# A slot-routing stage: the moments of one input taken a group earlier in each engine's queue

## The reference, cut to what matters

```python
x = x + mamba_layers(_layernorm(x), ...)      # ends in layernorm(r, norm_f_w, norm_f_b)
x = x + slots(_layernorm(x), ...)             # the first slot stage
x = x + attention(_layernorm(x), ...)
x = x + slots(_layernorm(x), ...)             # the second slot stage

def slots(x, ...):
    ctx = concatenate([x, slot_mean])
    h = gelu(ctx @ w1.T + b1)
    logits = (h @ w2.T + b2) / (abs(tau) + 0.1)
    alpha = top-8 softmax of logits over 64 slots
    slot_input = einsum('bts,btd->bsd', alpha, x) / alpha.sum(1)
    S_new = gru(slot_input, slots)
    return einsum('bts,bsd->btd', alpha, S_new @ wv.T + bv) @ wo.T + bo
```

## Time and profile before

| | us |
|---|---|
| median of 3 runs | 2447.85 (2445.73 to 2450.03) |
| the profiled execution, its own time | 2445.1 |
| its span in the profile | 2443.3 |
| first slot stage in it, from the end of Mamba to the start of attention | about 1765 to 1925 |
| second slot stage | from about 2349 |
| busy over the span: PE, DVE, ACT, POOL | 2114.9, 1886.0, 1785.2, 1636.1 |

### The profile page before, as it was taken

One profiled execution on the slowest core, in us unless ns is written; L12 is line 12 of the kernel. 1 busy time (PEld: TensorE's weight loads), 2 busy tenths in 40 slices (PEclk: granted clock), 3 DMA queues, 4 the chain that ended last, 5 costly groups with the idle time before them and its releaser, 6 DMA issues. The chain is left out here.

```text
span 2443.3 us, 40627 instructions
## 1 busy us (share of the span) xinstructions
PE 2114.9 (87%) x14680; PEld 1256.1 (51%) x14680; DVE 1886.0 (77%) x2590; ACT 1785.2 (73%) x3059; POOL 1636.1 (67%) x1436
## 2 busy tenths in 40 slices
PE   5989899898988989899898989988527599999977
PEld 2545545454554545455454554544324367666655
DVE  6888889888898888889888898988566455556555
ACT  3989898988989898998889889898333144444442
POOL 2888989898898988889898898989622123112120
PEclk9999999999999999999999999999857789999989
DMA  7240413405052341414324051331050301111032
GB/s 240 61 122 14 121 58 78 107 25 122 18 122 65 105 109 31 122 44 96 81 51 114 17 122 51 88 88 43 10 186 0 128 19 38 32 35 32 21 124 69
DMA packets 129788, 183.75 MB, mean 75 GB/s; under 512 B 14002, under 2 KB 75954, under 8 KB 129204
## 3 DMA queue, kind: packets, MB, share of 16 engines
q1 hardware_dynamic: 129588, 181.16, 27.6%
HBM read 134.45 MB, written 42.47 MB: 72 GB/s over the span
## 5 line engine op out<-in xcount | busy, mean ns | idle before, releaser
L620 POOL TENSOR_TENSOR h<-h,C_rep 128x512 f32<-128x512 f32 x1024 | 1275.5, 1280 | 195.2 <-ACT h_carry L529 195.2
L404 DVE TENSOR_TENSOR_SCAN h<-decay,h_carry,psum 128x512 f32<-128x512 f32 x768 | 955.4, 1269 | 126.8 <-PE psum L751 95.7
L521 ACT ACTIVATE decay<-dt_rep,A 128x512 f32<-128x512 f32 x1024 | 729.1, 712 | 97.3 <-DVE h L404 93.9
L751 PEld LDWEIGHTS psum<-ident,u_B 128*128 128x128 f32 x4096 | 478.9, 142 | 558.5 <-DVE h L404 306.6
L751 PE MATMUL psum<-ident,u_B 128*128 128x128 f32 x4096 | 632.9, 281 | 137.5 <-DVE h L404 105.5
L543 ACT ACTIVATE u_B<-u_tok,B_tok 128x512 f32<-128x512 f32 x832 | 588.9, 709 | 64.0 <-PE psum L751 46.3
L404 DVE TENSOR_TENSOR_SCAN h<-decay,zero,psum 128x512 f32<-128x512 f32 x256 | 318.6, 1269 | 50.0 <-PE psum L751 34.5
L762 PE MATMUL psum<-h,state_sum 128*32 128x512 f32 x2048 | 282.6, 625 | 10.9 <-POOL h L620 10.5
L609 POOL TENSOR_TENSOR u_B<-u_tok,B_tok 128x512 f32<-128x512 f32 x192 | 200.3, 1043 | 19.1 <-DVE u_tok L375 19.1
L674 PE MATMUL psum<-x_dt_gated,tap_diag 128*128 128x512 f32 x384 | 189.2, 597 | 0.0
L1578 DVE TENSOR_REDUCE a_row_max<-a_psum 128x4 f32<-128x512 f32 x128 | 87.7, 685 | 127.3 <-PE a_psum L1719 127.3
(11 more groups left out here) (207 smaller groups left out, 2757.3 us busy)
## 6 DMA issues: line engine op xcount, KB each, us to landing
dt_rep<-dt_rows SPq DMA_DIRECT2D x256, 256.0 KB, 5.6
C_rep<-C_rows SPq DMA_DIRECT2D x256, 64.0 KB, 2.0
dt_rows<-x_dt_gated SPq DMA_DIRECT2D x32, 512.0 KB, 5.0
residual<-mamba_residual SPq DMA_DIRECT2D x16, 512.0 KB, 3.9
mamba_residual<-residual SPq DMA_DIRECT2D x16, 512.0 KB, 2.9
x_tok<-mamba_residual SPq DMA_DIRECT2D x15, 512.0 KB, 4.5
f_gru_weights<-in_slot_gru_dram SPq DMA_DIRECT2D x2, 2176.0 KB
u_B<-in_x_dram SPq DMA_DIRECT2D x8, 512.0 KB, 9.3
```

Source lines behind the costliest of these rows:

```text
L404: dve.tensor_tensor_scan(h[:, slot(u)], dec[:, u % DEC], PS[:, u % 2], first, ALU.mult, ALU.add)\
L521: act.activation(dec[:, u % DEC], dtr[:, k % EG], ACT.Exp, scale=A[:, s // STEPS, k:k + 1]).then_inc(S["decay"], 1)
L620: pool.tensor_tensor(h[:, slot(u)], h[:, slot(u)], crep[:, k // EG], ALU.mult).then_inc(S["hc"], 1)
L751: ins = pe.transpose(PS[:, u % 2, tb * P:(tb + 1) * P], pr[:, f % 2, tb, eg], ident[:])
```

## The change

It changes the order of work in the first slot stage only. The moments of r of a group are now taken by DVE one group earlier than before, so that two groups of r are ahead at any time: `r_moments(0)` and `r_moments(1)` at the start, `r_moments(2)` before `combine(1)`, `r_moments(3)` before `combine(2)`. Two tables give the index of the moments in the new order, `R_AT` = 0, 1, 3, 5 for r and `X_AT` = 2, 4, 6, 7 for x. POOL serves the moments in that order. On ACT, `norm_r(1)` stands before `norm_x(0)`, and `norm_r(g + 2)` before `norm_x(g + 1)`. Without `normed` the order is as before.

```diff
+    R_AT = [max(2 * g - 1, 0) for g in range(G)]
+    X_AT = [min(2 * g + 2, 2 * G - 1) if normed else g for g in range(G)]
...
                 def norm_x(g):
-                    n = PER * g + PER - 1
+                    n = X_AT[g]
...
                 for g in range(G):
-                    for n in range(PER * g, PER * (g + 1)):
-                        rstd(n)
+                    if normed:
+                        for r in range(2) if g == 0 else range(g + 1, min(g + 2, G)):
+                            rstd(R_AT[r])
+                    rstd(X_AT[g])
                     norm_x(g)
...
                 def r_moments(g):
                     if g < G:
-                        moments(2 * g, rr, g, r_ld)
+                        moments(R_AT[g], rr, g, r_ld)
...
-                        moments(2 * g + 1, xa, g, None)
+                        moments(X_AT[g], xa, g, None)
...
                 if normed:
                     r_moments(0)
+                    r_moments(1)
                 else:
                     combine(0)
...
                 if normed:
-                    r_moments(1)
+                    r_moments(2)
                 combine(1)
-                if normed:
-                    r_moments(2)
                 dve.wait_ge(S["b2"], 1)
                 for g in range(G):
+                    if normed:
+                        r_moments(g + 3)
                     combine(g + 2)
                     top_k(g)
-                    if normed:
-                        r_moments(g + 3)
...
                 norm_r(0)
+                norm_r(1)
                 norm_x(0)
-                norm_r(1)
                 act.wait_ge(S["c1"], 1)
                 for g in range(G):
                     features(g)
+                    norm_r(g + 2)
                     norm_x(g + 1)
-                    norm_r(g + 2)
                     hidden(g)
```

More of the change, by code:

```diff
@@ L1110, in norm_r @@
                     if normed and g < G:
-                        n = 2 * g
+                        n = R_AT[g]
                         act.wait_ge(S["nm"], n + 1)
```

## The result

The changed kernel took 2426.7 us (median of 6 runs, 2419.32 to 2429.85) against 2446.51 (6 runs, 2435.66 to 2450.03) for the kernel before: ratio 0.9922, 95% interval 0.9899 to 0.9944. The profiled execution had a span of 2428.1 and a time of 2429.85.

What follows compares the result with a forecast made beforehand. DVE's queue, waiting 20.4 us for ACT's norm of r, was taken to bound the first slot stage. Gain 14.9 - 0.6 (POOL) - 1.5 (PE's clock) = 12.8 us, from 2447.85 to 2435.0; range 2430 to 2441.5.

Steps and rivals of the forecast that it cites:

- The sign: Whole kernel: faster 0.94, same 0.04, slower 0.02.
- 2431 or less with the tail at 2.4 GHz: Whole kernel: what is left after the rivals, a gain over 16 us; chance 0.03.
- a tail all at 1.2 GHz: From last L981 to last top-k: whole tail at PE's lower clock, costing 5.8 us, kernel 2439.3; chance 0.12.
- The bound and the chain: First slot stage: DVE's waits for ACT's norm of r set the chain; L981 of x group 3 comes 14.89 us earlier.
- The front: Start of the slot stage: DVE waits for r group 1's load, slot weights 6.76 us late, 3.19 of it net loss.
- ACT's order: ACT's queue, norm of r group 2 ahead of x group 1: delays x by 0 to 0.2 us, hidden; cost 0.
- POOL and DVE: Groups 1 to 3: POOL and DVE get in each other's way; cost 0.6 us, bounds 0 and 1.7.
- rival A: POOL is locked out through all three big DVE operations; gain only 9 us, kernel 2439; chance 0.18.
- PE's clock in the tail: Tail to the last top-k: likelier to begin at 1.2 GHz; cost 1.5 us, bounds 1.7 saved and 5.8 cost.
- The walk through PE's queue: PE's transposes, hidden and logits by group at the lower clock: PE just fits, about 1 us left; cost 0.
- The end of the range: Whole kernel: lower end 2430, from gains of 14.9 and 1.7 with 1 us for scatter of the median.
- the scatter of the median: Whole kernel: 1 us allowed for it in the lower end of the range, 2430.

Runs made afterwards that it cites:

- A late load: Changed kernel with the load of r group 1 issued after that of the GRU weights; ratio 0.9962 to the kernel before.
- the moments in the hole: Changed kernel, but moments of r group 1 taken inside the sum of group 0, between bias addition and product; ratio 0.9903 to the kernel before.
- the filled kernel before: Kernel before, with PE's idle times in the first slot stage filled by transposes of the identity that nothing waits for; ratio 1.0.
- the look-ahead for group 1 alone: Kernel before, with only the moments of r group 1 moved to the start, groups 2 and 3 left in place; ratio 0.9994.
- ACT's old order: Changed kernel, but ACT norms x group g+1 before r group g+2, and x 0 before r 1; ratio 0.9963 to the kernel before.

## Why the prediction came out as it did

**The sign: right. The chances: not.** Faster had 0.94, and faster it was. But the time lay outside the range, and what came, 2431 or less with the tail at 2.4 GHz, had been given 0.03, against 0.12 for a tail all at 1.2 GHz.

**The bound and the chain: right.** DVE's queue set the stage up to group 3. Its own steps, from the opening of the stage: L985 of x group 3 was forecast 14.89 earlier, with 0.6 taken off for POOL; 14.2 was measured. The difference of 0.7 is made up of: the front, 7.2 (L1052 at 17.6 after the opening, L1047 at 10.4 before) for 6.76, as the moments of r group 1 could begin 13.99 after the opening and not 13.59; two holds of L1004 by POOL, 2.56 instead of 2.29 twice, 0.5; and a gain not foreseen, that L1004 starts 0.08 before L1001 ends, three times, 0.2.

**The front: right, and the dearest part of the change.** A late load goes into the time one for one (7.8 us of wait, 7.7 of time), and the moments in the hole take 5.8 us off.

**ACT's order: right.** Its old order costs waits of 0.5, 2.0 and 1.6 us.

**POOL and DVE: right in size, and rival A fell.** The POOL timeline of the changed kernel:

```profile
1792.49 1.69 POOL L949 TENSOR_TENSOR f_rstd<-f_vareps,f_minushalf 128x8 f32<-128x8 f32 x1 [7.98 <-DVE f_vareps L985]
1794.26 1.37 POOL L951 TENSOR_TENSOR f_shift<-f_minusmean,f_rstd 128x8 f32<-128x8 f32 x1
...
1828.39 3.66 POOL L949 TENSOR_TENSOR f_rstd<-f_vareps,f_minushalf 128x8 f32<-128x8 f32 x1
...
1838.68 4.68 POOL L957 TENSOR_SCALAR f_xn<-f_x,f_rstd,f_shift 128x256 f32<-128x256 f32 x4
```

The power of 1828.39 was put off by the L1004 before it, 3.66 us for 1.63. Then four passes of 4.68 us, against DVE's L1001 of 1840.74 and L1004 of 1842.94 above: the last pass is over at 1843.36. So POOL was put off to the end of L1001, got in ahead of L1004, and L1004 was held 0.27 for it. It was not kept out through all three, as rival A had it. Of the exclusive lock in the Trainium skill ("SBUF — State Buffer", "Who interferes with whom") the trace shows both directions for the xn passes, but not for a power that is under way: L1001 of 1793.27 starts while the power of 1792.49 runs and takes 2.29 us as elsewhere. That a run of such DVE instructions would shut POOL out for its whole length is what I had made of it, and it isn't so.

**PE's clock in the tail: the step that failed.** The prediction put it as a cost of 1.5 us: hidden of group 2 would end sooner, PE would stand idle up to 5 us and enter the tail at 1.2 GHz. Measured was a gain of 1.65 (15.09 to 13.44), so the term is off by 3.15. The tail of the kernel before already began at the lower clock: its 16 transposes took 3.38 us in the earlier trace rows, where 1.97 does at 2.4 GHz. A low clock in the tail's first microseconds, which is what the term stood for, was in the 15.09 already, so it could add almost nothing, and its absence was a gain. PE in the changed kernel:

```profile
1843.42 1.97 PE L1200 MATMUL f_psum<-f_ident,f_xn 128*128 128x128 f32 x8 [1.58 <-POOL f_xn L957]
...
1848.49 6.04 PE L1212 MATMUL f_psum<-f_xn_feat,f_weights 128*128 128x512 f32 x8
1855.70 1.97 PE L1200 MATMUL f_psum<-f_ident,f_xn 128*128 128x128 f32 x16 [1.16 <-ACT f_xn L1126]
```

```profile
1849.00:1855.00 6.00, 5.54 (x8) 1.88 (x6) 5.86 (x36) 1.43 (x3) 3.20 (x4) 0.64 0.00 0
1855.50:1865.00 9.50, 9.30 (x58) 7.29 (x59) 4.71 (x31) 6.09 (x11) 0.68 (x2) 1.00 0.01 2
```

The second half of the transposes of group 2 waited 1.58 us for POOL's late pass; hidden of group 2 ran mostly at 1.2 GHz (6.04 us) and ended at 1854.53; the gap ahead of the tail was 1.16 us, and the granted clock of the tail was 1.00 against 0.85 in the earlier trace rows. The walk through PE's queue had found "about 1 us left" at the low clock, and the next step set it aside and took the gap as up to 5 us. Where that gap did come, in the kernel with the hole (5.96 us), the tail was 15.09, the same as before; so even then the cost over the kernel before was 0. That the clock makes this difference, and that PE's idle time in the stage sways it, is shown by the filled kernel before, where nothing else was changed. What is not shown is that the 1.16 us in place of the 2.07 are the reason: with 2.59 us, in the kernel with the look-ahead for group 1 alone, the tail also ran at 2.4 GHz. What decides the clock of the tail stays open.

**The end of the range.** With 15.9 us instead of 12.8 the same starting point, 2447.85, would have given 2432.0, inside the range: the clock term moved the forecast, but alone it would not have taken the time out of the range. The other 5.3 us are the measurement. The kernel before had a median of 2447.85 over 3 runs, 2446.51 over 6, 2442.24 over 20, 2442.5 over 11 and 2440.72 over 27, the last three on three different chips; the changed one 2426.7, 2428.31 and 2424.66. The 1 us that the prediction allowed for the scatter of the median was too little: the differences of the medians were 19.8, 13.9 and 17.8 for one and the same change. What makes the unchanged stages scatter by 2 to 11 us was not tried and stays open. It goes along with the granted clock: the changed kernel's runs of 2419.32 and 2429.85 us had 0.964 and 0.958.

**A version that beats both.** The moments of r group 1 in the hole of group 0: ratio 0.9903 (0.9883 to 0.9922) in its own measurement, 0.9947 and 0.9963 for the changed kernel and the one with ACT's old order in the same one.

## What to carry to other kernels

When work is moved ahead of a queue's first steps, look up when its data lands: here the advance put the front 7.2 us back, 3.6 of it work moved, and an idle slot of 2.3 us a few instructions later took up the same work for 1.3 us. For a serial tail on PE, first read from the rows at which clock it runs today, and take the gap ahead of it from the walk through PE's own queue, not guessed apart from it. Then put both clocks into the range: the same tail took 13.4, 15.1 and 16.75 us here, and the length of the gap didn't say which it would be. Of a change in one stage, compare the stage, from its first instruction on, since the stages that are the same differed from run to run by up to 10.6 us, two thirds of what was to be measured.

## What the runs showed of the hardware

A POOL xn pass that comes while DVE runs an addition of two operands in SBUF waits for its end and then gets in ahead of the next one, even where DVE's next one follows without a gap: four xn passes took 4.68 us for 2.18, and DVE's next operation 2.56 for 2.29. A power of POOL that is already under way does not hold such an addition: L1001 took 2.29 us beside the power of 1792.49, while POOL's next small product took 1.37 us for 0.20 and ended with it. PE's 16 transposes of group 3 took 1.91 to 1.97 us after gaps of up to 1.46 us without work, 3.38 to 3.63 after 2.02 and 2.07, 1.97 after 2.59, 2.51 after 3.31 and 3.62 after 5.96: the gap just ahead doesn't order them. The granted clock also fell to 0.50 inside work without a gap, in the first product of `gather` in the kernel before (5.33 us for 3.70).
